# Column orders of the inverse's levels in a gated delta layer: state reordered behind every second level, query half of A formed inside the levels

## The reference, cut to what matters

```python
def step(S, inp):
    qt, kt, vt, gt, bt = inp
    S = S * jnp.exp(gt)[..., None, None]
    kv = jnp.einsum('bhk,bhkv->bhv', kt, S)
    delta = (vt - kv) * bt[..., None]
    S = S + jnp.einsum('bhk,bhv->bhkv', kt, delta)
    o = jnp.einsum('bhk,bhkv->bhv', qt, S)
    return (S, o)
```

## Time and profile before

| | us |
|---|---|
| median of 3 runs | 241.28 |
| lowest, highest | 240.88, 242.41 |
| the profiled execution's own time | 241.87 |
| its span (first to last instruction) | 240.1 |
| PE busy | 226.5 (94%) |
| DVE busy | 135.7 (57%) |
| ACT busy | 133.7 (56%) |
| POOL busy | 105.0 (44%) |

### The profile page before, as it was taken

How to read it: one execution, slowest core, us unless ns; L and a number is a source line. 1 busy time by engine, 2 the same in 40 slices (tenths; PEclk the granted TensorE clock), 3 DMA queues, 4 the chain that set the end, 5 groups by cost and what they waited for, 6 DMA issues and landing times.

```text
span 240.1 us, 4086 instructions
## 1 busy us (share of the span) xinstructions
PE 226.5 (94%) x1513; PEld 190.6 (79%) x1513; DVE 135.7 (57%) x313; ACT 133.7 (56%) x248; POOL 105.0 (44%) x64
## 2 busy tenths in 40 slices
PE   8989999999999979789997999999999999999994
PEld 7646777777777777679875989975589999999994
DVE  3236555555555554633977466516234748977784
ACT  5145666666655555338865373637414859766570
POOL 1065566666666669130679930000000526555450
PEclk9999999999999999999999999999999999999999
DMA  6999999999999990999500000000000575980000
GB/s 208 389 426 410 419 419 414 419 417 420 419 419 388 419 381 5 337 427 418 218 0 4 0 0 3 0 0 4 0 0 0 179 270 206 411 332 11 0 3 22
DMA packets 8531, 52.92 MB, mean 220 GB/s; under 512 B 953, under 2 KB 1218, under 8 KB 6466
## 3 DMA queue, kind: packets, MB, share of 16 engines
q1 hardware_dynamic: 8514, 52.69, 54.9%
HBM read 52.56 MB, written 0.13 MB: 219 GB/s over the span
## 4 chain that ended last, share of the span: by engine, by line
PE 76%; DMA 6%; ACT 5%; DVE 5%; POOL 3%; issue 1%; SPq 1%; ACTq 0%; DVEq 0%; POOLq 0%
PE psum L420 35%; PE psum L488 14%; PE psum L714 8%; PE psum L415 7%; DMA late_sb<-in_ctx_T 6%; PE psum L605 3%; PE psum L613 2%; PE psum L411 2%; POOL work L395 2%; PE psum L638 1%; PE psum L665 1%; POOL ring L392 1%; PE psum L550 1%; DVE w_lo L1264 1%; PE psum L621 1%
## 5 line engine op out<-in xcount | busy, mean ns | idle before, releaser
L353 POOL TENSOR_TENSOR ctx_lo<-ring,ctx_hi 128x1792 fp32r<-128x1792 f32 x13 | 52.5, 4035 | 40.3 <-ACT ctx_hi L778 40.3
L403 POOL TENSOR_TENSOR h_lo<-ring,h_hi 128x512 fp32r<-128x512 f32 x16 | 24.8, 1548 | 69.6 <-ACT h_hi L949 63.6
L420 PE MATMUL psum<-late_sb,work 128*128 128x448 f32 x112 | 44.7, 542 | 1.7 <-DMA late_sb<-in_ctx_T 1.7
L420 PEld LDWEIGHTS psum<-late_sb,work 128*128 128x128 f32 x112 | 20.2, 190 | 18.6 <-issue 18.1
L785 ACT ACTIVATE probsT_hi<-psum 128x512 fp32r<-128x512 f32 (+1 forms) x28 | 13.7, 541 | 32.0 <-PE psum L415 32.0
L1009 DVE TENSOR_REDUCE smalls<-psum 128x1 f32<-128x896 f32 x14 | 15.3, 1092 | 23.6 <-PE psum L420 23.6
L420 PE MATMUL psum<-xT,late_sb 128*128 128x128 f32 x224 | 26.2, 276 | 0.1
L420 PEld LDWEIGHTS psum<-xT,late_sb 128*128 128x128 f32 x224 | 25.5, 192 | 0.3 <-DVE xT L1234 0.3
L778 ACT ACTIVATE ctx_hi<-ring 128x1792 fp32r<-128x1792 f32 x13 | 22.1, 1699 | 3.3 <-DMA ring<-in_ctx 3.3
L488 PE MATMUL psum<-ctx_hi,probsT_hi 128*128 128x256 f32 x98 | 20.6, 326 | 2.5 <-DVE probsT_lo L1033 2.5
L1033 DVE TENSOR_TENSOR probsT_lo<-psum,probsT_hi 128x512 fp32r<-128x512 f32 (+1 forms) x28 | 16.2, 619 | 7.4 <-ACT probsT_hi L785 7.4
(11 more groups left out here) (227 smaller groups left out, 412.8 us busy)
## 6 DMA issues: line engine op xcount, KB each, us to landing
late_sb<-in_ctx_T SPq DMA_DIRECT2D x14, 896.0 KB, 13.4
ring<-in_ctx SPq DMA_DIRECT2D x14, 896.0 KB, 12.0
late_sb<-in_late SPq DMA_DIRECT2D x10, 825.0 KB, 11.4
late_sb<-in_experts SPq DMA_DIRECT2D x8, 1024.0 KB, 6.2
late_slots<-in_experts SPq DMA_DIRECT2D x8, 1024.0 KB, 7.7
early_sb<-in_early SPq DMA_DIRECT2D x1, 512.0 KB, 4.1
early_sb<-in_early SPq DMA_DIRECT2D x1, 465.0 KB, 17.5
work<-in_levels SPq DMA_DIRECT2D x1, 416.0 KB, 19.2
```

What stands on the lines that cost most here:

```text
L353: nc.gpsimd.tensor_tensor(ctxNv[1][:, r % 2], ring[:, r], ctxNv[0][:, r % 2], ALU.subtract).then_inc(s["ctx_lo"], 1)
L403: nc.gpsimd.tensor_tensor(hT[1][:, e % 2, at, :], h32[:, at, :], hT[0][:, e % 2, at, :], ALU.subtract).then_inc(s["h_lo_done"], 1)
L420: last = nc.tensor.matmul(o, lhs(c), rhs(c), start=(c == 0), stop=(c == n - 1))
```

## The change

- The state's order is renewed behind levels 2, 4 and 6 in place of 3 and 6. The state moves through four buffers (`XL[(lv - 1) // 2]`, two places used in turn), and is read at step 1 in odd levels and step 2 in even ones (`state_columns`).
- The pairs keep their two buffers and their three orders: `pair_columns` reads them at step 1 in levels 1 and 4, step 2 in levels 2 and 5, step 4 in levels 3 and 6. `AL[0]` moves to the place that the scaled values `Bv` take later.
- ACT's `keep_columns` runs three times: (2) behind `copy_xt(2)` and ahead of the second SiLU of z, (4) behind `copy_xt(4)` and ahead of the second SiLU of the values, (6) as before. (3) is gone.
- The products of L613 go into the upper halves of banks 0 and 7, so that banks 1 and 2 keep the Gram products.
- DVE forms only the key half of `AW` ahead of the levels (eight instructions of 128x128). The eight of the query half stand inside levels 1 to 4, in each one behind the two L1154 and one behind the two L1164. TensorE waits for them (`aq_done`) ahead of L621.

```diff
-        XL = [R1[:, 4096:5120], R2[:, 6144:7168], R1[:, 4096:5120]]
-        AL = [R1[:, 2048:3072], R2[:, 2048:3072]]
-        X = XL[2].rearrange("p (h t) -> p h t", h=HV)
+        XL = [R1[:, 4096:5120], R2[:, 6144:7168], R1[:, 4096:5120], R2[:, 6144:7168]]
+        AL = [R1[:, 6144:7168], R2[:, 2048:3072]]
+        X = XL[3].rearrange("p (h t) -> p h t", h=HV)
...
+        def columns_at(t, b, shift, z):
 
             t = t[:, 512 * b:512 * b + 512]
-            if lv % 3 == 1:
+            if shift == 0:
                 return t.rearrange("p (f z i) -> p f z i", f=2, z=2)[:, :, z, :]
-            if lv % 3 == 2:
+            if shift == 1:
                 return t.rearrange("p (z i f) -> p z f i", f=2, z=2)[:, z, :, :]
             return t.rearrange("p (i f z) -> p z f i", f=2, z=2)[:, z, :, :]
 
-        def next_columns(t, b, z):
-
-            return t[:, 512 * b:512 * b + 512].rearrange("p (c f z i) -> p z f i c", c=2, f=2, z=2)[:, z, :, :, :]
+        def state_columns(lv, b, z):
+
+            return columns_at(XL[(lv - 1) // 2], b, (lv - 1) % 2, z)
+
+        def pair_columns(lv, b):
+
+            return columns_at(AL[(lv - 1) // 3], b, (lv - 1) % 3, 1)
+
+        def next_columns(lv, b, z):
+
+            return XL[lv // 2][:, 512 * b:512 * b + 512].rearrange("p (c f z i) -> p z f i c", c=2, f=2, z=2)[:, z, :, :, :]
...
-                        pe.wait_ge(s["xc_done"], b + 1)
+                    if lv in (3, 5):
+                        pe.wait_ge(s["xc_done"], lv - 3 + b + 1)
                     pe.wait_ge(s["x_done"], 2 * (lv - 1) + b + 1)
                     for f in range(2):
                         last = nc.tensor.matmul(bank[0 if b == 0 else 7][:, f * P:(f + 1) * P],
-                                                level_columns(pairs, b, lv, 1)[:, f, :], level_columns(state, b, lv, 0)[:, f, :], start=True, stop=True)
+                                                pair_columns(lv, b)[:, f, :], state_columns(lv, b, 0)[:, f, :], start=True, stop=True)
                     last.then_inc(s["t_mm"], 1)
-                    transposes([(bank[3 + b][:, f * P:(f + 1) * P], level_columns(state, b, lv, 1)[:, f, :]) for f in range(2)], s["xt_T"])
+                    transposes([(bank[3 + b][:, f * P:(f + 1) * P], state_columns(lv, b, 1)[:, f, :]) for f in range(2)], s["xt_T"])
...
-                        last = nc.tensor.matmul(bank[1 + b][:, g % 2 * P:(g % 2 + 1) * P], XT2[:, g, :], Tm[:, g, :], start=True, stop=True)
+                        last = nc.tensor.matmul(bank[0 if b == 0 else 7][:, (2 + g % 2) * P:(3 + g % 2) * P], XT2[:, g, :], Tm[:, g, :], start=True, stop=True)
...
-                pe.wait_ge(s["xc_done"], 2 + b + 1)
+                pe.wait_ge(s["xc_done"], 4 + b + 1)
+                pe.wait_ge(s["aq_done"], 4 * b + 4)
...
             copy_xt(2)
+            keep_columns(2)
             silu_z(1)
             copy_xt(3)
-            keep_columns(3)
             copy_xt(4)
+            keep_columns(4)
             silu_v(1)
...
+            def decay_gram(h, other):
+
+                kh = h // 2
+                return V.scalar_tensor_tensor(AW[:, h, other, :], bank[1 + kh // 2][:, (kh % 2) * 256 + other * P:(kh % 2) * 256 + (other + 1) * P],
+                                              s_("kap", h, h + 1), DT[:, h, :], ALU.mult, ALU.mult)
...
+                for h in range(4 * b, 4 * b + 4):
+                    decay_gram(h, 0).then_inc(s["aw_done"], 1)
...
+                if lv in Q_LEVELS:
+                    decay_gram(2 * lv - 2, 1).then_inc(s["aq_done"], 1)
                 for b in range(2):
                     dve.wait_ge(s["xx_mm"], 2 * (lv - 1) + b + 1)
-                    old = level_columns(state, b, lv, 0)
-                    step = bank[1 + b][:, 0:2 * P].rearrange("p (f i) -> p f i", f=2)
-                    if lv % 3 == 0:
-                        new, old, step = next_columns(XL[lv // 3], b, 0), split(old), split(step)
+                    old = state_columns(lv, b, 0)
+                    step = bank[0 if b == 0 else 7][:, 2 * P:4 * P].rearrange("p (f i) -> p f i", f=2)
+                    if lv % 2 == 0:
+                        new, old, step = next_columns(lv, b, 0), split(old), split(step)
                     else:
                         new = old
                     V.tensor_tensor(new, old, step, ALU.subtract).then_inc(s["x_done"], 1)
+                if lv in Q_LEVELS:
+                    decay_gram(2 * lv - 1, 1).then_inc(s["aq_done"], 1)
```

More of the change, by code:

```diff
@@ L26 @@
 V_LEVELS = (5, 6)
+Q_LEVELS = (1, 2, 3, 4)
 HIDDEN_BANKS = ((3, 4), (5, 6), (0, 7))
@@ L198, in perceiver @@
             consts_set warm_set eps_set
-            late2_in wqk_in dve_chain act_chain pool_chain conv_v y_free mx_done l_done out_ready x_ident al_low al_high kn_done xc_done
+            late2_in wqk_in dve_chain act_chain pool_chain conv_v y_free mx_done l_done out_ready x_ident aq_done al_low al_high kn_done xc_done
             var_done ln_sd ln_xn ln_T ln_xT q_ready q_done q_done_dve g_ready g_done g_done_act qb_ready qb_done bv_ready
@@ L217, in half @@
             return t[:, c * P:(c + 1) * P]
-        def level_columns(t, b, lv, z):
+        def columns_at(t, b, shift, z):
             t = t[:, 512 * b:512 * b + 512]
-            if lv % 3 == 1:
+            if shift == 0:
                 return t.rearrange("p (f z i) -> p f z i", f=2, z=2)[:, :, z, :]
-            if lv % 3 == 2:
+            if shift == 1:
                 return t.rearrange("p (z i f) -> p z f i", f=2, z=2)[:, z, :, :]
             return t.rearrange("p (i f z) -> p z f i", f=2, z=2)[:, z, :, :]
-        def next_columns(t, b, z):
-            return t[:, 512 * b:512 * b + 512].rearrange("p (c f z i) -> p z f i c", c=2, f=2, z=2)[:, z, :, :, :]
+        def state_columns(lv, b, z):
[4 more added lines that the diff above has]
+            return XL[lv // 2][:, 512 * b:512 * b + 512].rearrange("p (c f z i) -> p z f i c", c=2, f=2, z=2)[:, z, :, :, :]
         def low_order(t, b):
@@ L238, in high_order @@
             return t[:, 512 * b:512 * b + 512].rearrange("p (l h z) -> p h z l", l=64, h=4)
-        def level_state(lv):
-            return XL[(lv - 1) // 3], AL[(lv - 1) // 3]
         def split(t):
@@ L595, in _ @@
             for lv in range(1, LEVELS):
-                state, pairs = level_state(lv)
                 for b in range(2):
@@ L867, in keep_columns @@
                 for b in range(2):
-                    nc.scalar.activation(next_columns(XL[lv // 3], b, 1), split(level_columns(XL[lv // 3 - 1], b, lv, 1)), ACT.Copy).then_inc(s["xc_done"], 1)
+                    nc.scalar.activation(next_columns(lv, b, 1), split(state_columns(lv, b, 1)), ACT.Copy).then_inc(s["xc_done"], 1)
             for b in range(2):
@@ L1149, in _ @@
             for lv in range(1, LEVELS):
-                state = level_state(lv)[0]
                 mask = pair_masks[:, lv - 1:lv, :].to_broadcast([P, 2, P])
```

## The result

The changed kernel takes 242.26 us (median of 22 runs, 241.32 to 243.97), the kernel before 241.32 us in 22 runs beside it. The ratio is 1.0039, with a 95% interval of 1.0025 to 1.0053: slower by 0.94 us, well inside 1%. I had forecast 241.7, which was +0.43 us on its median.

The account below looks back on a forecast made before the run. TensorE, busy 94% of the span, was taken to bound the kernel, except for ACT stretches at levels 1 and 5. Terms -0.3 up to copy_xt(4), +1.13 ACT, -0.38 level 6 were summed as +0.43: 241.7 us, range 239.9 to 242.9.

Parts of the forecast that it names:

- Ahead of the levels: DVE's shorter work before level 1: done 1.08 us sooner, counted as 0 because level 1 waits behind ACT's L852.
- Query half and banks: Query pieces inside levels 1 to 4 cost 0.05 us in sum; L613's shared banks cost 0.
- Level 2's scattered write: State update ending level 2 now scatters its writes: 0.76 us to the next load instead of 0.47, +0.29.
- Level 3: Level 3: -0.38 us from L605's products, -0.25 from the update no longer scattering its writes.
- once the moving operand is cheap, the load sets the pace: L605 in levels 3 and 6: load needs 0.21 us, batch 0.85 instead of 1.04, four batches -0.76.
- The bound above it: L605 in levels 3 and 6: at most -2.4 us if the load falls to step 1's pace.
- Step 2 in level 4: Level 4's state read at step 2 instead of 1: two batches and their transposes cost about +0.05 us.
- ACT's pair (4): keep_columns(4) between copy_xt(4) and L852, where ACT has no pause until copy_xt(5): +1.13 us.
- free loads: Rival at L605: loads are free of the step, 1.6 us more saved, 240.1 us; chance 0.17.
- The unchanged pace: Rival at L605: level 3's spacing stays above 0.23, products save nothing, +1.2, 242.5 us; chance 0.10.
- ACT's pair is covered: Rival at level 5: kernel held elsewhere or pair cheaper at step 2, down to -0.7, 240.6 us; chance 0.07.
- the front is worth its 1.1 us: Rival ahead of the levels: DVE's shorter work counts, 240.6 us, needs POOL to end earlier; chance 0.05.

Follow-up runs that it names:

- the second: Changed kernel with ACT doing copy_xt(5) before the second value half's SiLU, table load and square root, value scaling behind level 6: 241.54 us, 1.0004 to the kernel before.
- the first run: Kernel before with only A's query half formed inside levels 1 to 4, L613's products in banks 0 and 7, first pair layout moved: 241.38 us, ratio 0.9995.

## Why the prediction was right, and where its terms were off

The direction and the range were right, and the largest term had the right cause; the sum was 0.5 us short of the 0.94 measured. (Its terms as written add up to +0.46, not +0.43.) That it came this near is partly luck: the products' saving was taken 0.35 too large, ACT's cost 0.2 too large, which hid half of that, and the 0.29 was missing. By the steps of the prediction:

- **Ahead of the levels: 0.** Right, shown by the part alone (0.9995). The bound "up to 1.08 us" if the cover went was too high: uncovered it is 0.58.
- **Query half and banks: 0.05.** Measured 0.00 in the part alone. In level 3 of the changed kernel the update follows its query piece at once, but TensorE isn't kept from anything by it.
- **Level 2's scattered write: +0.29.** Right: level 2 became longer by 0.31 us. From the update's start (132.85) to the next level's first load (133.64) it is 0.79 us, where I had put 0.76.
- **Level 3: -0.63 in products and write.** It became 0.40 shorter: 0.22 up to L613's first product, for which I had put 0.38, and 0.18 behind it, for which I had put 0.25. Level 6 shows the products alone, without a change of its write: -0.19 instead of -0.38. The step that was off is "once the moving operand is cheap, the load sets the pace": the load by itself needs 0.233 us a record where I read 0.21, which is the pace of both operands (0.235) within 1%, and the -0.11 a batch comes from the batch's start and the transposes. The bound above it, the load at the pace of step 1, did not come, and the run with the pairs at step 1 shows that the step is worth 1.87 us to the end. The Trainium skill's rule in "TensorE: Matmul & The Clock Gate" (section on LDWEIGHTS), columns over 1.2 GHz, has no term for a step; the rows disagree with it at step 4. The Trainium skill's "SBUF — State Buffer" (section Specifications) says that SBUF has lines of 16 bytes and wants two hits or more in each for full bandwidth. The rows here agree, if that is held to loads as well as to moving operands: fp32 at step 2 has two elements in a line and costs next to nothing (0.118 us a load against 0.112), at step 4 it has one and the pace doubles.
- **Step 2 in level 4: +0.05.** Nothing of it shows: from level 4's first product to ACT's second copy of `copy_xt(4)` it is 1.74 us before and 1.73 after. Level 4 as a whole became longer by 0.16, all of it behind that copy, at the scattered write, which I had counted as hidden behind ACT, and it is: the wait for `copy_xt(5)` follows it.
- **ACT's pair (4): +1.13.** From `copy_xt(4)` to `copy_xt(5)` it was 2.41 us before (140.59 to 143.00) and is 3.34 after (139.02 to 142.36): +0.93. The mechanism is shown by the run with the late SiLU. The size was 0.2 too large: I took 1.23 us for the pair and 0.1 for its overlap with the next instruction, and it is 1.11 long and gives the queue free after 0.91 (139.30 to 140.21). With the read step at 2 the changed kernel's pairs of `keep_columns` take 1.11 to 1.19 us and not 1.23 to 1.25 as before, so "a smaller read step will not cheapen it" was wrong by a tenth of a microsecond for ACT.
- **What I did not have: +0.29 on ACT**, 13 us behind the levels, from two instructions more. It is a third of the measured loss. I had followed every instruction that was added up to the levels' end and had no row that prices a shift of the program.

Sum by the traces: -0.11 up to `copy_xt(4)`, +0.93 ACT, -0.19 level 6, which makes the 0.62 of the levels within 0.02, and 0.29 behind them: 0.91.

Of the rivals, free loads fell with the 0.233. The unchanged pace did not fall: its sign was a spacing in level 3 above 0.23, and that is what came, 0.233 against 0.235. Only its price was wrong, since 0.11 us a batch was saved beside the pace; the measured 242.26 lies nearer to its 242.5 than to my 241.7, though it holds the 0.29 on ACT that neither had. "ACT's pair is covered" and "the front is worth its 1.1 us" fell with the second and the first run. TensorE's granted clock stayed at 1.00 through the longer wait in level 5.

The last kernel beats both: 238.86 us against 241.33. It has the change, three layouts of the pairs, both value SiLUs where ACT has a pause, and two idle copies that move ACT's program past the gap.

## What to carry to other kernels

- Where two streams run side by side, price each operand's access by itself before cleaning one: at step 4 either of them held the pace, and taking one away brought 0.11 us of 1.04, taking both 0.59.
- Moving work into an engine's list is free only in a pause of that list. Look from the place of insertion to the next instruction that another engine waits for; a table load in between makes the stretch solid.
- When a change of under 1% is to be explained, align the traces at a point ahead of it. The spans alone had the sign wrong here.

## What the runs showed of the hardware that I had not expected

- A fp32 load of 128 columns at step 4 holds a pace of 0.233 us a record, with 0.21 between the first two of a batch; at step 1 it is 0.112, at step 2 0.118. The transposes' loads take 0.20 to 0.22 us at step 4, about 0.20 at step 2 and 0.14 at step 1, yet at step 4 too the load behind a pair of them starts 0.13 us after the second.
- ACT started one instruction 0.34 us late in each of the eight kernels with two instructions more ahead of it, and in none of the five with zero or four.
